# A two-layer state-space, mixture-of-experts and attention kernel on one core: gate logits as two products per tile, kernel taps four heads at a time, and a new order of VectorE work

## What is computed

```
xn = layernorm(x)
x  = x + ssm(xn) + moe_top2(xn)          # layer 0
xn = layernorm(x)
x  = x + attention(xn) + moe_dense(xn)   # layer 1

# ssm: a long convolution along the sequence, with 1024 taps per head computed from A, C, dt:
K  = 2 * real(einsum('hn,hnl->hl', Ct, V));  y = irfft(rfft(x) * rfft(K))[:L]
# moe_top2: 8 experts of 341, the two best of 8 gate logits, softmax over the two
# attention: softmax over axis 1 of q k^T / sqrt(128), then attn^T v
# moe_dense: 8 experts of 512, every token through all of them
gate = softmax(x @ Wg + bg);  thr = sigmoid(x @ Wt + bt) * 0.125
w = (gate - thr) * ((gate - thr) >= 0);  w = w / sum(w)
h = gelu(x @ W1[e] + b1[e]);  out = sum_e w[e] * (h @ W2[e] + b2[e])
```

## Time and profile before

| | |
|---|---|
| median of 3 runs | 863.48 us (863.02 to 864.82) |
| profiled execution: its own time | 863.7 us |
| profiled execution: span | 861.7 us |
| busy share of the span, PE / PEld / DVE / ACT / POOL | 91 / 71 / 75 / 66 / 22 % |
| mean granted clock of TensorE | 0.948 of full speed |

### The profile page before, as it was taken

The page is one execution under the profiler, slowest core; times in us unless marked ns, Lnnn a source line. Parts: engine busy times, 40 slices in busy tenths (PEclk is TensorE's granted clock), DMA queues, the critical chain, the costliest instruction groups (busy, mean ns, idle before and its releaser), DMA issues.

```text
span 861.7 us, 11941 instructions
## 1 busy us (share of the span) xinstructions
PE 781.5 (91%) x4082; PEld 614.0 (71%) x4082; DVE 643.5 (75%) x1456; ACT 569.3 (66%) x1010; POOL 191.3 (22%) x246
## 2 busy tenths in 40 slices
PE   7967714999999987999999999999999998999998
PEld 6625713666666643787887888788888886999997
DVE  7699545688853848978987997687777777777775
ACT  5842111455555547779979987899999995665664
POOL 0068774167766750001100000000000000000000
PEclk9977557899999999999999999999999999999999
DMA  8644672387776533434421221221222100000000
GB/s 270 231 144 156 201 225 63 118 248 238 235 238 199 175 127 48 80 68 100 86 43 40 54 49 38 37 53 48 49 49 49 49 25 1 13 13 20 13 19 25
DMA packets 79466, 84.89 MB, mean 99 GB/s; under 512 B 11248, under 2 KB 63728, under 8 KB 79152
## 3 DMA queue, kind: packets, MB, share of 16 engines
q1 hardware_dynamic: 68688, 70.71, 28.4%
q0 software_dynamic: 6496, 12.92, 5.9%
q10 hardware_dynamic: 4224, 0.52, 0.4%
HBM read 59.72 MB, written 24.41 MB: 98 GB/s over the span
## 4 chain that ended last, share of the span: by engine, by line
PE 58%; DVE 3%; ACT 3%; POOL 1%; issue 1%; DVEq 0%; ACTq 0%; POOLq 0%
PE ps L1794 17%; PE ps L1796 17%; PE ps L1795 17%; PE ps L2122 3%; PE ps L1983 3%; POOL y_rows L675 1%; DVE hid_lo L1708 1%; ACT hid L919 1%; ACT hid_hi L920 0%; PE ps L2148 0%; ACT L919 0%; ACT L895 0%; PE ps L1960 0%; DVE xn L1439 0%; ACT prob L944 0%
## 5 line engine op out<-in xcount | busy, mean ns | idle before, releaser
L1708 DVE TENSOR_TENSOR hid_lo<-hid,hid_hi 128x512 fp32r<-128x512 f32 x256 | 176.6, 690 | 70.6 <-ACT hid_hi L920 66.5
L919 ACT ACTIVATE hid<-ps,b_sb 128x512 f32<-128x512 f32 x256 | 177.4, 693 | 41.2 <-PE ps L1796 21.7
L920 ACT ACTIVATE hid_hi<-ps,b_sb 128x512 fp32r<-128x512 f32 x256 | 175.6, 686 | 0.0
L1794 PE MATMUL ps<-hid_hi,w_lo 128*128 128x512 f32 x256 | 101.2, 396 | 6.1 <-DVE hid_lo L1708 6.0
L1794 PE MATMUL ps<-xt_hi,w_lo 128*128 128x512 f32 x256 | 102.5, 400 | 1.2 <-DVE xn L1439 1.2
L1796 PE MATMUL ps<-xt_hi,w_hi 128*128 128x512 f32 x256 | 100.1, 391 | 0.0
L1796 PE MATMUL ps<-hid_hi,w_hi 128*128 128x512 f32 x256 | 100.0, 391 | 0.0
L1795 PE MATMUL ps<-xt_lo,w_hi 128*128 128x512 f32 x256 | 100.0, 391 | 0.0
L1795 PE MATMUL ps<-hid_lo,w_hi 128*128 128x512 f32 x256 | 99.9, 390 | 0.0
L675 POOL DMA_INDIRECT y_rows<-yo,row_of x76 | 81.4, 1071 | 67.1 <-issue 62.7
L633 POOL DMA_INDIRECT x_slots<-xn,slot x64 | 72.1, 1126 | 62.6 <-DVE expert_of L1195 43.4
(11 more groups left out here) (333 smaller groups left out, 1680.3 us busy)
## 6 DMA issues: line engine op xcount, KB each, us to landing
gate_row<-gates_dram SPq DMA_DIRECT2D x64, 256.0 KB, 4.9
wc<-w_split SPq DMA_DIRECT2D x19, 768.0 KB, 5.8
w_split<-wc SPq DMA_DIRECT2D x8, 768.0 KB, 4.9
x_slots<-prod SPq DMA_DIRECT2D x11, 520.0 KB, 10.8
xc<-x_slots SPq DMA_DIRECT2D x19, 260.0 KB, 2.8
wst<-w SPq DMA_DIRECT2D x16, 256.0 KB, 4.3
wd<-w SPq DMA_DIRECT2D x19, 192.0 KB, 2.7
acc<-y_rows POOLq DMA_DIRECT2D x14, 256.0 KB, 4.9
```

Of the source, the lines that this page charges most:

```text
L919: nc.scalar.activation(hid1[:, u % 4], ps[:, u % 4], ACT.Gelu_apprx_tanh, bias=b1_sb[:, u:u + 1])
L920: nc.scalar.activation(hid1_hi[:, u % 4], ps[:, u % 4], ACT.Gelu_apprx_tanh, bias=b1_sb[:, u:u + 1]).then_inc(hid1_done, 1)
L1708: tt(hid1_lo[:, u % 4], hid1[:, u % 4], hid1_hi[:, u % 4].bitcast(F32), sub).then_inc(hid1_lo_done, 1)
L1794: mm(dst, a_lo, b_hi, start=first, stop=False)
```

## The change

It has five parts.

- **Taps.** The 16 heads of a chunk are taken four at a time (`HG = 4`): a 64x128 by a 64x128 operand gives a 128x128 output, of which the four 32x32 blocks on the diagonal are the taps and the rest is not used. There are 16 products of 128 columns per chunk where there were 64 of 32. The copy takes all 128 partitions, and each half is stored with four DMAs of 16 KB where it was one of 64 KB.
- **Order of DVE ahead of the chunks.** The second half of the `khat` sums moves behind `input_low(0)` and `input_low(1)`, the derived parts of `khat` behind the first two `hidden`, and the 12 early products are gone: each chunk now has up to 7 products in place of 6 (3 before `hidden(q+1, 0)`, 4 after it), and all 96 are in chunks 0 to 13.
- **Table.** ACT applies silu to one column before the first `input_high`.
- **Gate logits of layer 1.** The high and low weights lie side by side in `wg1_parts`. Per tile there are two products, hi times 20 columns and lo times 10 columns, and DVE adds the two halves with a second instruction.
- **Order in layer 1, group 0.** `scale_rows(1)`, `scale_rows(2)`, `gate_thresholds(0)` and `gate_weights(0)` move from ahead of the first unit into units 0 to 3, and most of the steps that stood in units 0 to 31 move back by one to five units, on PE by two.

```diff
-EARLY = 2 * PAIR - 14 * 6
-PER_CHUNK = 6
+PER_CHUNK = 7
+HG = 4
...
+        wg1_parts = sb("wg1_parts", [P, 2, GW], F32R)
...
-                sp.wait_ge(k_stored[n], 16 * KC)
+                sp.wait_ge(k_stored[n], 16 * HG * KC)
...
+            copy(wg1_parts[:, 0], wsmall[:, P:]).then_inc(ws_hi_done, 1)
...
-                    copy(k_out[:, c % 2, half], ps[0:LO, k_bank(c) + half].rearrange("p (a b) -> p a b", a=CH)).then_inc(k_copied, 1)
+                    copy(k_out[:, c % 2, half], ps[:, k_bank(c) + half]).then_inc(k_copied, 1)
                 act_e.wait_ge(k_copied, 2 * c + 2)
                 for half in range(2):
                     heads = half * HH + c * CH
-                    act_e.dma_start(kernel_dram[heads:heads + CH].rearrange("j m n -> m j n"),
-                                    k_out[:, c % 2, half]).then_inc(k_stored[c % 2], 16)
+                    dst = kernel_dram[heads:heads + CH].rearrange("(i a) m n -> a m i n", a=HG)
+                    for a in range(HG):
+                        src = k_out[a * LO:(a + 1) * LO, c % 2, half].rearrange("m (i b n) -> m i b n", b=HG, n=LO)
+                        act_e.dma_start(dst[a], src[:, :, a]).then_inc(k_stored[c % 2], 16)
...
             act_e.wait_ge(rows_in, 48)
+            nc.scalar.activation(newton[:, 0:1], eps[:], ACT.Silu)
             input_high(0, 0)
...
-                    if is_at(g, u, 0, 27):
+                    if is_at(g, u, 0, 28):
                         gate_exp(1)
...
+            tt(wg1_parts[:, 1], wsmall[:, P:], wg1_parts[:, 0].bitcast(F32), sub).then_inc(ws_lo_done, 1)
...
-            for i in range(EARLY):
-                product(i)
...
-                first = EARLY + (turn or 0) * PER_CHUNK
+                first = (turn or 0) * PER_CHUNK
...
+            spectrum_sums()
+            dve.wait_ge(rows_in, 48)
+            v = step.mark(ts(vec_rows[:, 0], vec_rows[:, 0], 1.0, 1.0 / C, add, mul))
+            need(v)
+            khat_sums(0)
             input_low(0, 0)
             input_low(1, 1)
+            khat_sums(1)
             hidden(0, 0, 0)
             hidden(0, 0, 1)
+            khat_parts()
             all_chunks(dve, chunk_hidden)
...
-                tt(gl[:, t], ps[:, 6 + g % 2, 0:B * GW].rearrange("p (t e) -> p t e", e=GW),
-                   bias1[:].unsqueeze(1).broadcast_to((P, B, GW)), add).then_inc(logits1_read, 1)
+                parts = ps[:, 6 + g % 2, 0:2 * B * GW].rearrange("p (t a e) -> p t a e", a=2, e=GW)
+                v = step.mark(tt(gl[:, t], parts[:, :, 0], bias1[:].unsqueeze(1).broadcast_to((P, B, GW)), add))
+                need(v)
+                tt(gl[:, t], gl[:, t], parts[:, :, 1], add).then_inc(logits1_read, 1)
...
-            scale_rows(1)
-            scale_rows(2)
-            gate_thresholds(0)
-            gate_weights(0)
...
+                if at(0, 0): gate_thresholds(0)
+                if at(0, 1): gate_weights(0)
                 if at(0, 2):
+                    scale_rows(1)
+                    layer0_sum(1)
+                if at(0, 3):
+                    scale_rows(2)
                     gates_copy(0)
+                if at(0, 4):
                     layer0_sum(2)
+                    unit_stats(1)
+                if at(0, 5):
+                    unit_moments(1)
+                    unit_stats(2)
...
+                if at(0, 9): unit_normalise(1, 1)
+                if at(0, 13): unit_normalise(2, 1)
...
+                if at(1, 0): gates_copy(1)
...
-                    for h in range(CH):
-                        o = ps[0:LO, k_bank(c) + half, h * LO:(h + 1) * LO]
-                        mm(o, high[states, 0, c * CH + h], low[states, 0, c * CH + h], start=True, stop=False)
-                        last = mm(o, high[states, 1, c * CH + h], low[states, 1, c * CH + h], start=False, stop=True)
+                    for i in range(CH // HG):
+                        o = ps[:, k_bank(c) + half, i * P:(i + 1) * P]
+                        heads = slice(c * CH + i * HG, c * CH + (i + 1) * HG)
+                        for part_ in range(2):
+                            factors = (a[states, part_, heads].rearrange("p h l -> p (h l)") for a in (high, low))
+                            last = mm(o, *factors, start=(part_ == 0), stop=(part_ == 1))
...
-                    o = ps[:, 6 + g % 2, b * GW:(b + 1) * GW]
-                    w = slice(GATE1, GATE1 + GW)
-                    last = three(o, xt1_hi[:, g, c], xt1_lo[:, g, c], ws_hi[:, w], ws_lo[:, w])
+                    o = ps[:, 6 + g % 2, 2 * b * GW:2 * (b + 1) * GW]
+                    mm(o, xt1_hi[:, g, c], wg1_parts[:].rearrange("p a e -> p (a e)"), start=True, stop=False)
+                    last = mm(o[:, 0:GW], xt1_lo[:, g, c], wg1_parts[:, 0], start=False, stop=True)
...
-                if at(0, 0): gates_turn(0)
-                if at(0, 10):
+                if at(0, 2): gates_turn(0)
+                if at(0, 12):
                     pe.wait_ge(gates1_copied, 1)
                     turn1(1)
-                if at(0, 15):
+                if at(0, 17):
...
```

More of the change, by code:

```diff
@@ L38 @@
 UN1 = E * J1
-QK, V1, GATE1 = 0, P, 2 * P
+QK, V1 = 0, P
 STAGES = 3
@@ L110, in program @@
         WCOLS = 2 * E * HID1
-        SCOLS = 2 * P + GW + 6
+        SCOLS = 2 * P
         ws_hi = sb("ws_hi", [P, SCOLS], F32R)
         ws_lo = sb("ws_lo", [P, SCOLS], F32R)
+        wg1_parts = sb("wg1_parts", [P, 2, GW], F32R)
         xn = sb("xn", [P, T, RW])
@@ L772, in _ @@
             act_e.wait_ge(ws_in, 32)
-            copy(ws_hi[:, V1:V1 + P + GW], wsmall[:]).then_inc(ws_hi_done, 1)
+            copy(ws_hi[:, V1:V1 + P], wsmall[:, 0:P]).then_inc(ws_hi_done, 1)
+            copy(wg1_parts[:, 0], wsmall[:, P:]).then_inc(ws_hi_done, 1)
             def w0_high(e):
@@ L1354, in product, with khat_sums @@
                 op.then_inc(products_done, 1)
-            spectrum_sums()
-            dve.wait_ge(rows_in, 48)
-            v = step.mark(ts(vec_rows[:, 0], vec_rows[:, 0], 1.0, 1.0 / C, add, mul))
-            need(v)
-            for m in range(HM):
+            def khat_sums(m):
                 dve.wait_ge(khat_copied, 2 * m + 2)
@@ L1369, in _, with khat_parts @@
                 step.mark(stt(im, im, 2.0, im2, mul, add))
-            need(step.n)
-            for m in range(M):
-                o_re, o_im = (sub, add) if m in (0, M - 1) else (add, sub)
-                v = step.mark(tt(khat[:, m, 0], khat[:, m, 0], vec_rows[:, 0], add))
-                need(v)
-                tt(khat[:, m, 2], khat[:, m, 2], khat[:, m, 1], o_re).then_inc(khat_ready, 1)
-                tt(khat[:, m, 3], khat[:, m, 3], khat[:, m, 0], o_im).then_inc(khat_ready, 1)
-            dve.wait_ge(khat_ready, 2 * M)
-            for i in range(EARLY):
-                product(i)
+            def khat_parts():
+                need(step.n)
+                for m in range(M):
+                    o_re, o_im = (sub, add) if m in (0, M - 1) else (add, sub)
+                    v = step.mark(tt(khat[:, m, 0], khat[:, m, 0], vec_rows[:, 0], add))
+                    need(v)
+                    tt(khat[:, m, 2], khat[:, m, 2], khat[:, m, 1], o_re).then_inc(khat_ready, 1)
+                    tt(khat[:, m, 3], khat[:, m, 3], khat[:, m, 0], o_im).then_inc(khat_ready, 1)
+                dve.wait_ge(khat_ready, 2 * M)
             def chunk_hidden(q, k, s, left, turn):
-                first = EARLY + (turn or 0) * PER_CHUNK
+                first = (turn or 0) * PER_CHUNK
                 steps = range(first, min(first + PER_CHUNK, 2 * PAIR)) if turn is not None else ()
@@ L1988, in _ @@
             pe.wait_ge(inv_in, 16)
-            pe.wait_ge(ws_lo_done, 1)
+            pe.wait_ge(ws_lo_done, 2)
             for g in range(G - 1):
@@ L2022, in next_groups @@
                 at = lambda g_, u_: (g, u) == (g_, u_)
-                if at(0, 0): gates_turn(0)
-                if at(0, 10):
+                if at(0, 2): gates_turn(0)
+                if at(0, 12):
                     pe.wait_ge(gates1_copied, 1)
                     turn1(1)
-                if at(0, 15):
+                if at(0, 17):
                     pe.wait_ge(part1_done, 3)
                     turn1(2)
-                if at(0, 17): logits1(1)
-                if at(0, 21): logits1(2)
-                if at(0, 29): gates_turn(1)
+                if at(0, 19): logits1(1)
+                if at(0, 23): logits1(2)
+                if at(0, 31): gates_turn(1)
                 if at(1, 26):
```

36 lines of the change are left out of this document (15 added, 21 removed).

## The result

The changed kernel took 855.73 us (median of 6 runs, 853.06 to 856.7) against 863.51 for the kernel before in the same rounds: ratio 0.9899, 95% interval 0.9886 to 0.9911, so 7.8 us or 1.0% faster. The forecast was 853.3 us, in a range of 849.5 to 858.5. The profiled execution took 855.35 us, its span is 853.4 (861.7 before).

The account below looks back on a forecast made before the run. PE bounds the layer 1 experts, a chain of waits the stretch ahead of the chunks; 5.0 + 2.2 + 2.9 = 10.1 us off the 861.7 us span gives a median of 853.3 us, range 849.5 to 858.5.

Parts of the forecast that it names:

- The head start at the chunks: Ahead of the chunks: `input_low(0)` starts 6.86 us earlier, less 1.85 us paid back in stalls, worth 5.0 us.
- stalls of 1.85 us: First chunks: PE waits for DVE 1.1 us at `up(1, 1)` and 0.75 us more at `up(2, 0)`.
- rival 2: At the chunks TensorE's clock stays up, `xct_lo` of chunk 2 done at 160.1: 2.2 us more gain, 851.1 us; chance 0.14.
- Seven products for six: In the chunks: a seventh product takes 0.61 of DVE's 0.64 us idle, PE still sets the pace: 0 us.
- rival 1: DVE becomes the bound of the chunks: 855.9 us, or 858.4 if all the head start is paid back; chance 0.14.
- The taps: Ahead of the chunks: PE time unchanged, read-back issued some 2 us later but covered by 3.7 us: 0 us.
- cover of 3.7 us: Ahead of the chunks: the taps' path, ending with the last `khat` copy, is 3.7 us ahead of the rows' path.
- Rival 3: The 32 tap stores hold the taps back and the kernel is slower, 868.1 us; chance of the stores 0.07.
- The start of the experts: Layer 1, group 0: new DVE order brings PE's `down1` of unit 10 from 360.97 to 358.8, worth 2.2 us.
- later copy of the gates: Groups 1 and 2: copy one DVE slot later; if late by 1 us, DVE would wait and PE not yet.
- rival 4: The new order in group 0 gives nothing since some step waits for one that moved: 855.5 us; chance 0.09.
- Gate logits: Layer 1 experts: four fewer small products save 0.42 us a group, 2.9 us for seven groups.

## Why the prediction came out as it did

*The head start at the chunks (5.0 us)* was right in its mechanism up to the second turning: from the order I expected 6.86 us there, and it is 6.91. Of the stalls of 1.85 us that I took off, 0.4 came in the changed kernel. What followed was not the forecast but rival 2: the clock stayed up, and `up(2, 0)` came at 158.11, 9.3 us earlier, 0.1 after an `xct_lo` done at 158.0, where rival 2 says 160.1 less the 1.55 that the rows were early. It is not a fixed property of the change: of the eight profiles with both the new order and the new taps three had the clock at 2.4 GHz there, three at 1.2 GHz for 3.4 us, and two for 6.8. The `yt` copy of chunk 0 starts 13.5 to 13.8 us after the first turning in the first kind, 14.9 to 15.1 in the second and 16.8 to 17.0 in the last, so it is worth up to 3 us there. At the end of the loop 1.3 of it were left in the one pair of kernels with the same loop (the changed one and that of the gates at unit 31): where POOL is the bound, a late start of PE is partly made up. That the forecast of this term came out all the same, 4.8 us at the last chunk for 5.0, is luck: 1.55 us of early rows and the clock went one way, the loop the other. The Trainium skill, TensorE: Matmul & The Clock Gate, section Part 1: The HAM clock gate (the "warmup" mystery), has free-running windows, and that the same code meets either case agrees with it.

*Seven products for six (0 us)* is the step that failed. DVE did fit, with a little more room than I read: besides the 0.64 us of rows 6 it had sat idle for 0.20 before another `hidden` of that chunk (185.22). But I had DVE's time alone in view. POOL does its four copies and four scatters beside it, and its rounds of 7.5 to 8.9 us were already above PE's 7.62 in much of the old loop. The loop got 5.4 us longer, not 0 (3.5 to 5.4 over the four profiles, against 140.1), by the chain: unbroken products on DVE, longer POOL copies and scatters, later `rows_known`, SP's queue, late `wc`, PE, and once the lower clock behind PE's wait. It was cut at three links: without products the loop is 12.2 us shorter, with half the copies 9.6, with the weight load ahead of the wait 4.8, each by one profile and against the longest of the four loops; in the time these are 4.9, 8.3 and 2.7 us. Which DVE instruction holds which copy was read from the timelines, not tried. In size this is rival 1, in mechanism it isn't: PE waited for DVE 0.9 us, and with half the copies and the same work on DVE the loop is 4.2 us shorter than the old one. The Trainium skill, SBUF — State Buffer, section Who interferes with whom, says that a DVE instruction with two inputs in SBUF contends with a GpSimd one that reads SBUF. The products have two such inputs, and the copies of 0.19 us that become 0.44 or 1.61 agree with it; no run here changes where the inputs lie.

*The taps (0)* cost 1.5 us in the old order (0.3 to 2.6), by a path that the profiles leave open. The 32 stores took 0.46 us in the median and landed in 3.7, but the read-back came 6.9 us later than before and not 2. The last store was issued at 117.95 and ended 2.2 us later than I had worked out, and it landed 6.7 us after its start: I had used the median of 3.3, where the last one decides, and even before that one took 5.2. The read-back then landed in 3.5 us instead of 8.3, which is why it did little harm. The cover of 3.7 us was nearly gone: in the changed kernel the last `khat` copy ended at 140.80 and the rows were turned at 141.55, and in the kernel with two POOL copies the first turning, at 142.77, waited for that copy, with its rows landed from 140.73 on. Rival 3's price never came near.

*The start of the experts (2.2)* was 1.8 us at unit 10, near what I had worked out, and about 1.1 by the end of group 0. I had said of the later copy of the gates that DVE would wait and PE not yet. DVE waited 1.6 us, and that came through: with the copy back at unit 31 1.8 to 2.5 us return. The step left out is the chain behind the copy, a store, its landing and a load, 1.9 to 3.7 us from the store's issue to the load's alone over all profiles. Taken by itself this part gave nothing, as rival 4 has it.

*Gate logits (2.9).* A block takes 0.81 us (0.83 expected): 20 columns cost what 10 cost. But two of the seven blocks lie in group 0, where DVE sets the pace, so five count: 5 x 0.44 = 2.2 us, and 2.2 is what the profile of this part alone has at the end of the last group. In the time it is 3.6 (2.4 to 4.8).

*The sum* on the spans: at the last normalisation (334.40, before 338.99) the changed kernel is 4.6 us ahead (forecast 5.0), up to the end of group 0 it gains 1.1 more (forecast 2.2) and behind it 2.6 (forecast 2.9): 8.3 us, where I had 10.1.

## What to carry to other kernels

When work is moved onto an engine that has room, look at what the engines beside it do in that time and whether their instructions get longer, and at each queue that waits for them: here two tiny copies on POOL were worth about as much on the first chip as the whole change (8.3 and 7.8 us). A head start is only as good as the slowest engine of the loop behind it, so list the round of every engine, POOL's and SP's too, and compare it with PE's before and after. A wait of 3 us of PE can cost nearly 5, as its clock may fall behind it (237.0 to 240.4 us here). And a step whose result goes through memory must keep its place in time even when its consumer seems some units away.

The best kernel measured on the first chip is the changed one with POOL's copies joined (847.6 us, 2.0% less than before); with the gates of groups 1 and 2 copied out where they were the span was another 1.5 us shorter, on the second chip.

## What the hardware showed that I had not expected

On the second chip the old form of the taps ran very slowly. PE's timeline of the kernel before with joined POOL copies, and the first chip's of the kernel before, for the same products:

```profile
126.94 0.21 PE L1855 MATMUL ps<-low,high 64*32 64x32 f32 x1 [1.89 <-issue]
127.65 0.25 PE L1856 MATMUL ps<-low,high 64*32 64x32 f32 x1 [0.50 <-issue]
129.04 0.21 PE L1856 MATMUL ps<-low,high 64*32 64x32 f32 x1 [1.14 <-issue]
```

```profile
81.28 0.29 PE L1860 MATMUL ps<-low,high 64*32 64x32 f32 x2
81.39 0.29 PE L1859 MATMUL ps<-low,high 64*32 64x32 f32 x2
```

From 82 to 135 us the products come singly or a few at a time, with pauses of 0.3 to 2.6 us between them in which PE waits for nothing that the profile shows, instead of one instruction every 0.05 us; from 140 us on it does 204 instructions in 10 us. The last `yt` lies 32 us later than before. The three kernels with a quarter as many, larger products show none of it on that chip, and there the change was worth 44 us and not 8; that the old taps account for the difference is read from this one profile, not tried. Its cause is open. The kernel before took 889 us or more in all 11 runs on that chip.
